# Graph attention on one core: SyncE fetches 20 of the 1564 tiles of K and V rows, one transfer per row

## What is computed

```python
q = (x @ Wq + bq).reshape(N, 8, 16)            # k and v in the same way
scores = sum(q[dst] * k[src], axis=-1) / 4 + (edge_attr @ We + be)
e = exp(scores - segment_max(scores, dst)[dst])
probs = e / (segment_sum(e, dst) + 1e-10)[dst]
agg = segment_sum(probs[:, :, None] * v[src], dst)
out = layernorm(x + agg @ Wo + bo)
```

## Time and profile before

| | |
|---|---|
| time, median of 3 runs | 2427.78 us (2426.92 to 2436.58) |
| span of the profiled execution | 2449.4 us |
| granted TensorE clock, mean | 0.786 of full speed |
| POOL busy, gathers | 1496.0 us, 1536 |
| PE, DVE, ACT busy | 1545.6, 1370.8, 454.6 us |
| memory traffic | 117 GB/s over the span |

### The profile page before, as it was taken

How to read it: one execution, slowest core, us unless ns; L and a number is a source line. 1 busy time by engine, 2 the same in 40 slices (tenths; PEclk the granted TensorE clock), 3 DMA queues, 4 the chain that set the end, 5 groups by cost and what they waited for, 6 DMA issues and landing times.

```text
span 2449.4 us, 25231 instructions
## 1 busy us (share of the span) xinstructions
PE 1545.6 (63%) x6655; PEld 1051.5 (43%) x6655; DVE 1370.8 (56%) x3214; ACT 454.6 (19%) x1496; POOL 1496.0 (61%) x1572
## 2 busy tenths in 40 slices
PE   5354576657665757566656666566766666666566
PEld 4233454435343434444444444344444444444344
DVE  4254575656555655555655656555555555556556
ACT  1011121212121211111111212111211212111112
POOL 4736546666666666666666666666666666666661
PEclk7677788868778777877887887877878778788878
DMA  6423334343334334343434343434334343434331
GB/s 248 160 84 105 94 101 130 107 123 115 118 117 130 109 108 130 107 131 108 129 108 128 111 129 108 128 108 125 112 113 127 110 128 111 126 111 127 108 106 31
DMA packets 115143, 288.11 MB, mean 118 GB/s; under 512 B 45909, under 2 KB 53856, under 8 KB 107960
## 3 DMA queue, kind: packets, MB, share of 16 engines
q0 software_dynamic: 74624, 203.26, 28.3%
q1 hardware_dynamic: 37628, 76.52, 9.4%
q10 hardware_dynamic: 2748, 6.69, 0.7%
HBM read 274.69 MB, written 11.67 MB: 117 GB/s over the span
## 4 chain that ended last, share of the span: by engine, by line
PE 40%; issue 25%; another core or an unknown queue 14%; DVE 10%; POOL 9%; DMA 1%; ACT 1%; DVEq 0%; ACTq 0%; POOLq 0%
PE ps_q L1230 14%; PE ps_a L1266 11%; POOL kv_buf L523 9%; PE ps_e L1242 2%; PE ps_t L1216 2%; PE ps_t L1210 2%; DVE prod L850 1%; DVE score L860 1%; DMA kv_buf<-kv_table,src_i 1%; PE ps_s L1294 1%; DVE wv L870 1%; PE ps_a L1319 1%; DVE run_fwd L912 1%; PE ps_a L1320 1%
## 5 line engine op out<-in xcount | busy, mean ns | idle before, releaser
L523 POOL DMA_INDIRECT kv_buf<-kv_table,src_i x1536 | 1465.6, 954 | 899.6 <-issue 407.5
L1230 PE MATMUL ps_q<-q_blk,hots 128*128 128x256 f32 x1564 | 566.4, 497 | 553.8 <-issue 553.6
L1230 PEld LDWEIGHTS ps_q<-q_blk,hots 128*128 128x128 f32 x1564 | 351.9, 246 | 677.7 <-issue 625.2
L1266 PE MATMUL ps_a<-wv,hots 128*128 128x272 f32 x1564 | 559.9, 490 | 8.5 <-issue 5.6
L613 ACT ACTIVATE hots<-ps_t 128x512 f32<-128x512 f32 x377 | 225.1, 597 | 1784.8 <-remote 1035.1
L850 DVE TENSOR_TENSOR prod<-ps_q,kv_buf 128x512 f32<-128x512 f32 (+1 forms) x392 | 268.7, 685 | 497.8 <-remote 322.7
L870 DVE TENSOR_TENSOR wv<-kv_buf,ps_w 128x512 f32<-128x512 f32 (+1 forms) x392 | 266.3, 679 | 238.8 <-remote 179.5
L1266 PEld LDWEIGHTS ps_a<-wv,hots 128*128 128x128 f32 x1564 | 335.4, 238 | 61.0 <-issue 10.4
L860 DVE TENSOR_REDUCE score<-prod 128x32 f32<-128x512 f32 (+1 forms) x392 | 267.2, 682 | 7.9 <-issue 0.2
L930 DVE TENSOR_TENSOR_SCAN ps_s<-seq_far,seq_left,ps_s 8x512 f32<-8x512 f32 x57 | 72.7, 1275 | 188.0 <-remote 155.0
L1309 PE MATMUL ps_a<-sums_sb,carry_from 128*1 128x136 f32 x112 | 28.0, 342 | 195.2 <-DVE sums_sb L982 154.8
(11 more groups left out here) (157 smaller groups left out, 1398.1 us busy)
## 6 DMA issues: line engine op xcount, KB each, us to landing
edge_f<-in_edge_blk SPq DMA_DIRECT2D x55, 1024.0 KB
kv_buf<-kv_table,src_i POOLq DMA_INDIRECT x1536
kv_table<-kv_buf ACTq DMA_DIRECT2D x12, 512.0 KB, 3.2
xt_blk<-in_x_t SPq DMA_DIRECT2D x114, 32.0 KB
out<-y_out SPq DMA_DIRECT2D x114, 32.0 KB
kv_buf<-in_x_perm SPq DMA_DIRECT2D x5, 512.0 KB
codes<-code_table SPq DMA_DIRECT2D x108, 10.5 KB
code_table<-kv_buf SPq DMA_DIRECT2D x1, 1344.0 KB
```

The costliest lines, as they stand in the source:

```text
L523: pool.indirect_dma_start(kv_buf[:, b % NBUF, t, :], None, kv_table, bass.IndirectOffsetOnAxis(ap=src_i[:, column:column + 1], axis=0)).th ...
L1230: one = pe.matmul(ps_q[q % 2][:, k * 2 * D:(k + 1) * 2 * D], hots[:, (v - 1) % 2, 0, k * P:(k + 1) * P], q_blk[:, b % QBUF, :], start=True ...
L1266: one = pe.matmul(sums(b), hots[:, (v - 1) % 2, 1, k * P:(k + 1) * P], wv[:, q % 2, 2 * k:2 * k + 2, :].rearrange("p j w -> p (j w)"), sta ...
```

## The change

After the change, the four tiles of step 6 of blocks 10, 20, 30, 40 and 50 are no longer gathered by POOL. SP fetches them, one plain DMA of 1 KB per row: 5 blocks x 4 tiles x 128 rows = 2560 transfers. They go to a ring of three places in `x_first`, which block 0 has done with by then. DVE computes the byte offsets of these rows once in the setup (`src_at`, five small instructions). SP loads the four offsets of a partition into four registers with one instruction, and issues four transfers. In each of its iterations 0 to 49 it does 13 partitions, which makes 52 transfers, until the 640 partitions are done (in iteration 49 there are 3 left). From iteration 3 on they stand between the two stores: `store` is split in two calls. `multiply` and `weigh` take these five steps from the ring, and `multiply` waits for the transfers of the ring's place. POOL's gathers skip the 20 tiles; its waits and their values for other steps are as before.

```diff
@@ -8,6 +8,7 @@
 F32R = mybir.dt.float32r
 BF16 = mybir.dt.bfloat16
 I32 = mybir.dt.int32
+U8 = mybir.dt.uint8
 ALU = mybir.AluOpType
 ACT = mybir.ActivationFunctionType
 AX = mybir.AxisListType
@@ -52,6 +53,12 @@
     FIRST_TILE = [sum(TILES[:b]) for b in range(NB + 1)]
     SLOT = 7
     LAG = 5
+
+
+    BY_ROW, RING = 52, 3
+    EVERY = -(-QUAD * P // BY_ROW)
+    ROW_BLOCKS = list(range(EVERY, NB - 4, EVERY))
+    ROW_STEP = {(b, SLOT - 1): k for k, b in enumerate(ROW_BLOCKS)}
     XAHEAD = 3
 
     HELD, AHEAD = 6, 2
@@ -129,6 +136,7 @@
         x_first = sb("x_first", [P, T, D])
         xt_first = sb("xt_first", [P, 2, QUAD * P])
         src_i = sb("src_i", [P, NT], I32)
+        src_at = sb("src_at", [P, len(ROW_BLOCKS), QUAD], I32)
         neg_rel = sb("neg_rel", [P, NT])
         base_bc = sb("base_bc", [P, NH])
         carry_from = sb("carry_from", [P, NH])
@@ -191,6 +199,8 @@
         chk = edge_f[:, :, :].rearrange("p a e -> p (a e)")
         chk_i = chk[:, 0:NT + 1].bitcast(I32)
         chk_f = chk[:, NT + 1:2 * NT + 1]
+        ring = x_first[:, 0:RING * 2 * QUAD, :].rearrange("p (i t a) d -> p i t (a d)", i=RING, t=QUAD)
+        table_bytes = kv_table.rearrange("n d -> (n d)").bitcast(U8)
         row_less = run_max[0:ROWS, 13:15]
         dst_i = neg_rel[:, :].bitcast(I32)
         ends_dst = in_kv(ENDS, 2, 24, SEQ + 1).bitcast(I32)
@@ -269,6 +279,8 @@
         s_x = [sem(f"s_x{i}") for i in range(XBUF)]
         s_kv = [[sem(f"s_kv{i}_{g}") for g in range(SLOT)] for i in range(NBUF)]
         s_y = sem("s_y")
+        s_srcat = sem("s_srcat")
+        s_rows = [sem(f"s_rows{i}") for i in range(RING)]
 
 
         s_setup = sem("s_setup")
@@ -344,6 +356,13 @@
 
             return [by_head(a, n).rearrange("p h (s j) -> p j h s", j=2)[:, j] for j in range(2)]
 
+        def kv_of(b, g):
+
+            t0, t1 = STEP[b][g]
+            if (b, g) in ROW_STEP:
+                return ring[:, ROW_STEP[b, g] % RING]
+            return kv_buf[:, b % NBUF, t0:t1, :]
+
         def columns(b, t0, t1):
             return slice(FIRST_TILE[b] + t0, FIRST_TILE[b] + t1)
 
@@ -452,17 +471,32 @@
                 sync.dma_start(seq_far[:, b % 2, 0:SEQ], far_table[b:b + 1, :].to_broadcast([H, SEQ])
                                ).then_inc(s_seqi[b % 2], 16)
 
-            def store(b):
-                sync.wait_ge(s_normal, b + 1)
-
-                for j in range(2):
-                    first = sync.value_load(first_row[0:1, 2 * b + j:2 * b + j + 1], min_val=0, max_val=N)
-                    if b + j >= 1:
-                        sync.wait_ge(s_y, 16 * (2 * b + j))
-                    sync.dma_start(out[bass.ds(first, W), :], y_out[j * W:(j + 1) * W, b % 2, :]).then_inc(s_y, 16)
+            def load_rows(lo, hi):
+
+                for r in range(lo, min(hi, len(ROW_BLOCKS) * P)):
+                    k, p = divmod(r, P)
+                    if p == 0 and k >= RING:
+                        sync.wait_ge(s_weighted, FIRST[ROW_BLOCKS[k - RING]] + SLOT)
+                    _, at = nc.values_load_multi_w_load_instructions(
+                        src_at[p:p + 1, k, :], engines=[mybir.EngineType.SP], min_val=0, max_val=(NR - 1) * KV * 4,
+                        skip_runtime_bounds_check_because="sources are node numbers, as the gathers take them")
+                    for t in range(QUAD):
+                        sync.dma_start(ring[p:p + 1, k % RING, t, :].bitcast(U8), table_bytes[bass.ds(at[t], KV * 4)]
+                                       ).then_inc(s_rows[k % RING], 16)
+
+            def store(b, j):
+                if j == 0:
+                    sync.wait_ge(s_normal, b + 1)
+                first = sync.value_load(first_row[0:1, 2 * b + j:2 * b + j + 1], min_val=0, max_val=N)
+                if b + j >= 1:
+                    sync.wait_ge(s_y, 16 * (2 * b + j))
+                sync.dma_start(out[bass.ds(first, W), :], y_out[j * W:(j + 1) * W, b % 2, :]).then_inc(s_y, 16)
 
             general = is_general(sync)
             with sync.If(general == 0):
+                sync.wait_ge(s_srcat, 1)
+                sync.wait_ge(s_xturned, GS[0])
+                some = BY_ROW // QUAD
                 for b in range(NB + 3):
                     if b == 0:
                         load_seq(0)
@@ -475,7 +509,10 @@
                         load_codes(b + 1)
                         load_seq(b + 1)
                     if b >= 3:
-                        store(b - 3)
+                        store(b - 3, 0)
+                    load_rows(b * some, (b + 1) * some)
+                    if b >= 3:
+                        store(b - 3, 1)
                 sync.wait_ge(s_y, 32 * NB)
             with sync.Else():
                 for b in range(min(XAHEAD, NB)):
@@ -509,6 +546,8 @@
                                pattern=[[-1, P]], channel_multiplier=1).then_inc(s_setup, 1)
             def gather(b):
                 for g, (t0, t1) in enumerate(STEP[b]):
+                    if (b, g) in ROW_STEP:
+                        continue
                     if b >= NBUF:
                         pool.wait_ge(s_weighted, steps_over(b - NBUF, t1))
                     q = FIRST[b] + g
@@ -810,6 +849,10 @@
             dve.tensor_tensor(ends_far, ends_dst[:, 1:SEQ + 1], ends_dst[:, 0:SEQ], ALU.not_equal).then_inc(s_far, 1)
             dve.wait_ge(s_far, FAR_OF_ENDS["changes"])
             dve.tensor_scalar(ends_far, ends_far, FAR, None, ALU.mult).then_inc(s_far, 1)
+            dve.wait_ge(s_src, 16)
+            for k, b in enumerate(ROW_BLOCKS):
+                one = dve.tensor_scalar(src_at[:, k, :], src_i[:, columns(b, *STEP[b][SLOT - 1])], float(4 * KV), None, ALU.mult)
+            one.then_inc(s_srcat, 1)
             dve.wait_ge(s_chk, 16)
             dve.tensor_tensor(chk_f, chk_i[:, 1:NT + 1], chk_i[:, 0:NT], ALU.is_lt).then_inc(s_win, 1)
             dve.wait_ge(s_win, WIN["falls"])
@@ -842,14 +885,18 @@
                 dve.wait_ge(s_byedge, q + 1)
                 if b == 0:
                     dve.wait_ge(s_staged, len(HALVES) + 2 * g + 2)
+                elif (b, g) in ROW_STEP:
+                    k = ROW_STEP[b, g]
+                    dve.wait_ge(s_rows[k % RING], 16 * QUAD * P * (k // RING + 1))
                 else:
-                    landed = sum(STEP[k][g][1] - STEP[k][g][0] for k in range(b % NBUF, b + 1, NBUF) if k and g < GS[k])
+                    landed = sum(STEP[k][g][1] - STEP[k][g][0] for k in range(b % NBUF, b + 1, NBUF)
+                                 if k and g < GS[k] and (k, g) not in ROW_STEP)
                     dve.wait_ge(s_kv[b % NBUF][g], 16 * landed)
                 if q >= 2:
                     dve.wait_ge(s_dot, q - 1)
                 dve.tensor_tensor(prod[:, q % 2, 0:n * D].rearrange("p (t d) -> p t d", d=D),
                                   ps_q[q % 2][:, 0:n * D].rearrange("p (t d) -> p t d", d=D),
-                                  kv_buf[:, b % NBUF, t0:t1, 0:D], ALU.mult).then_inc(s_product, 1)
+                                  kv_of(b, g)[:, :, 0:D], ALU.mult).then_inc(s_product, 1)
 
             def dot(q):
                 b, g = STEPS[q]
@@ -869,7 +916,7 @@
                     dve.wait_ge(s_summed, q - 1)
                 dve.tensor_tensor(
                     wv[:, q % 2, 0:t1 - t0, 0:D].rearrange("p t (h d) -> p t h d", d=HD),
-                    kv_buf[:, b % NBUF, t0:t1, D:KV].rearrange("p t (h d) -> p t h d", d=HD),
+                    kv_of(b, g)[:, :, D:KV].rearrange("p t (h d) -> p t h d", d=HD),
                     by_head(ps_w, TILES[b])[:, :, t0:t1].rearrange("p h (t a) -> p t h a", a=1)
                     .to_broadcast([P, t1 - t0, H, HD]), ALU.mult).then_inc(s_weighted, 1)
```

## The result

The changed kernel takes **2650.0 us** (median of 4 runs, 2641.1 to 2657.4), the kernel before 2428.5 (median of 4): a ratio of 1.089, with an interval of 1.086 to 1.093. So it is slower, by 221.5 us, where 84 were forecast. The two profiled spans, 2449.4 and 2650.3 us, differ by 200.9.

The account below looks back on a forecast made before the run. No engine was full; the loop was taken as bound by engines waiting for each other, POOL fullest with its pauses. POOL's -5 us and +89 us for late codes gave +84 us, 2512 us, range 2408 to 2780 us.

Parts of the forecast that it names:

- Mechanism: On SP the rows stand ahead of the codes, which come 1.9 us late in 47 passes, holding PE: +89 us.
- the price of SP's pass: SP's 13 register loads and 52 transfers in an iteration were put at 31.1 us, taken as 31 us.
- the eight tiny transfers on ACT: Back to back on ACT they took 3.04 us, 0.38 each; with the MOVE 0.41, giving 26.9 us for SP's iteration.
- rival 3: SP runs at 0.7 us for half of its instructions: some 54 us an iteration, +1170 us, 3600 us; chance 0.09.
- Room by order: Slack on SP from codes landing at 1217.6 to the match that needs them, in one pass: 29.2 us.
- The check by throughput: SP's waits for `y_out` (22.9 us) and before `load_seq` (9.2) leave 32.1 us of a 40.7 us block: 31 just fits.
- The bound that was to turn the sign: A row's price on SP of 0.45 us: above it the kernel is slower, below it the same or faster.
- POOL's -5 us: 20 gathers fewer save 25 us of POOL's time; 1 us was taken as gained at each of five places.
- two samples: Waits of DVE's multiply in step 6: block 20 waited for data, 2.16 us; block 40 for PE, 7.21 us.
- Rival 2: POOL is the pace after all, each skipped step gives its 5 us: -15 to -25 us, 2403 to 2413 us; chance 0.18.
- rival 1: SP keeps up and POOL's 5 us are not missed: only -5 us remain, 2423 us; chance 0.35.
- nothing on DVE: Five small setup instructions on DVE add at most 1.8 us, taken as 0; `multiply` and `weigh` cost as before.

## Why the prediction was wrong in size and right in kind

**Mechanism: right in kind.** The rows stand ahead of the codes, the codes land late, PE waits for them (498.6 us in 46 times where "once in a block" was forecast), and SP's wait for `y_out` is gone while there are rows. The experiment with the codes alone moved shows this cause on the later occasions: 58 of 68 us. What sets the size of the loss in the first measurement is another matter; there SP has no idle time left, and its own sum is the pace.

**The step that failed first is the price of SP's pass**, 31.1 us, from 0.49 us a row and 0.434 us a load. In the first measurement it was 39.2 us between the stores, 0.73 us a row with its share of the loads. On the later occasions it was 26.6. That the estimate by the eight tiny transfers on ACT had 26.9 is in part luck: a load takes 0.565 us there, not 0.434, and a transfer with its MOVE 0.34 us, not 0.41. The figure of about 600 ns in the Trainium skill (DMA: Bandwidth & Descriptors, Latency and other measured facts) is therefore nearer for this form, which loads four registers, than the median that I took from a form that loads one. The stretches with 0.7 us for an instruction were seen in the trace of before and set aside, as in rival 3, as a case of all or nothing. They were there in part: the median row was quick and the mean was not. A mean over a stretch of SP would have said it, a median hides it.

**The second is how the delay adds up.** Room by order was put at 29.2 us, from one pass and with 1.9 + 0.4 us for landing and match. The trace of before has 32.6 us from the issue of the codes to the first multiply in the mean, and 6.7 of them are needed: 25.9 us of room. With 39.2 us that would make 13.3 us a block by the working of the prediction, 47 x 13.3 = 625 us in all. It was 4.0 us a block. For past the point where SP has no idle time left, the delay in one pass isn't added to the next; the block just becomes as long as SP's iteration, 45.7 us, and 45.3 were measured. The check by throughput, which the prediction made and then passed over as the looser one, is what sets the end. It too was off: it gives 40.7 - 32.1 + 39.2 = 47.8 us for a block. The 32.1 took a wait of 9.2 us before `load_seq` for each block, which 24 blocks had; and SP's other work, 8.6 us a block by that sum, was 6.5 us in the changed kernel (45.7 less 39.2). The runs with 64 rows show the same on a later occasion, 38.1 us for an iteration and 38.3 for a block. That the order would have mended little in the first measurement follows from this; it was not shown there.

**The bound that was to turn the sign** was 29.2 us for all rows of an iteration, 0.45 us a row with the loads apart, and the forecast was to fall under 29 us between the stores. It didn't hold: on the later occasions 52 rows took 26.6 us, and the kernel was still 2.1% slower. Worked out from means, the room there is 30.7 us of lead in the kernel before, less the 7.6 that are needed, 23.1 us. The stores stand 22.7 us apart with 44 rows, which were faster, and 26.6 with 52, which were slower.

**POOL's -5 us.** In the first measurement the five blocks with fewer gathers are shorter by 1.9 to 3.8 us than the mean of 45.3 in four cases, and block 50, at 32.0, by 13; with SP as the pace that says nothing on POOL. On the later occasions the whole 25.7 us come, when SP lets them. That two samples gave 1 us of 5 was a reading of the first condition: about half of the idle time of DVE's multiply (270 of 492 us) and of POOL (266 of 498 us), its pauses left out, fell there into silences of PE. And one of the two was misread. In step 6 of block 40 PE had spread the step's queries by 1779.32, before its silence:

```profile
1778.29 1.03 PE L1230 MATMUL ps_q<-q_blk,hots 128*128 128x256 f32 x4
```

The multiply at 1787.76 still stands ahead of PE's next instruction, at 1789.90. It didn't wait for that product, and what ended its 7.2 us is not shown. Rival 2 was the case on the later occasions. The rule of the Trainium skill behind rival 1 (DMA: Bandwidth & Descriptors, Issuing engines are not separate DMA queues) didn't decide: issue time was all that was saved, and issue time was the pace.

**Right as put:** nothing on DVE (1372.1 us busy against 1370.8); the rows in time, since no kernel shows a wait of DVE for their landing. That all else behind the rows is free was nearly right: it cost some 10 us on the later occasions.

**What stays open** is the first condition: 406 us more for the same program, with silences of PE and 0.7-us instructions. None of the fifteen runs made later met it, and its cause was not found. It doesn't follow the granted clock: one of the four runs of the changed kernel has 1.0 on record and took 2657.4 us, the others 0.757 to 0.759 and 2641.1 to 2652.1.

## What to carry to other kernels

Before giving an idle queue more work, write its iteration out twice: once as a sum against the period (throughput), and once as the chain from what releases it to what is needed next (order). Put the new work behind every transfer that someone waits for: the same 2560 transfers cost 68 us in one place and nothing in another. Past the sum, no order helps (with 64 rows it cost 1.6%), and a price per item has to be taken as a mean over a stretch, not as the median of one instruction. The version with the rows behind the loads beats both kernels, 1996 us against 2022 and 2064; its gain is all POOL's, 1.3 us for each tile that it doesn't gather.

## What was not expected of the hardware

- The same program and data took 2428 us in one measurement and 2022 in four others on four chips, in the profiles with PE busy for 1545.6 and 1367.6 us at a mean granted clock of 0.786 and 0.843. A kernel's bound can change with that: POOL, idle for 899.6 us in the one profile, was the pace of the kernel before in the other, idle for 473.0 us that are its pauses.
- A small transfer on SP has two prices: 0.30 us at a fixed address, 0.48 us at an address from a register, loads included (one load for four rows, 0.565 us).
- Two transfers that wait for each other cost SP 2.5 to 3 us for the pair, while with 25 us of other work between them the second costs 0.5.
